# A Mamba block, an attention block and two expert layers: the hand-over into each expert search, and the first expert behind it

## The chip, the core and the metric

One core of a Trainium2 chip runs the whole program. The metric is the device time of one execution in microseconds (us); lower is better.

## The reference, cut to what matters

The input x is 16 sequences of 512 tokens with 256 channels, float32 (8192 tokens).

```python
x = x + mamba(layernorm(x))        # d_inner 512, 16 states, conv width 4
x = x + ffn(layernorm(x))
x = x + attention(layernorm(x))    # linear attention, 16 heads, chunks of 128
x = x + ffn(layernorm(x))

def ffn(x):                        # 8 experts, hidden 512
    capacity = n // 8              # 1024 tokens for each expert
    scores = (x_flat @ Wg.T).T     # (8, 8192): the gate products
    top_vals, token_idx = top_k(scores, capacity)
    token_w = softmax(top_vals)
    xg = x_flat[token_idx]
    h = silu(xg @ W1.T) * (xg @ W3.T)
    y = (h @ W2.T) * token_w[..., None]
    return zeros.at[token_idx].add(y)
```

## The kernel before

There are four stages: `mamba` (prefix m), `moe` (f), `attention` (t), `moe` (g). A counter `done` is raised at the end of each, and every engine waits for it before the next. The two layers with tokens in order (m, t) walk over the 16 batches (one sequence of 512 tokens each, four tiles of 128 tokens); the order of the work on every engine is written out by hand, and work of three neighbouring batches is interleaved: while batch b runs its scans or its attention, batch b-1 gets its output norm, its transposes and its gate products, and batch b+1 its input products. Behind each batch, `residual` adds the block's output to x, `out_norm1/2` (m) or `out_stats` (t) take mean and variance on VectorE, GpSimd makes `rstd` and `nm` of them in four small steps (a power and three others), ScalarE writes the normalized rows `xn1t`, TensorE transposes them (`ptr`), ScalarE copies the transposes out, and TensorE multiplies them with the gate's weights (`gate_scores`) into four groups of 32 partitions, one for each tile.

The search of `moe` wants the scores in another layout: `sc` has 128 partitions, partition 16e + b for expert e and batch b, with that batch's 512 tokens in a row. For batches 0 to 14 the scores go through HBM (`scores`), and `search.early`, issued from SyncE's queue near the end of m or t, loads them and the search's constants. In t it begins when the scores of batch 14 have landed in HBM, and behind it in the same queue stand the stores of the last batch (L1957, L1959). For batch 15, four DMAs (two from SyncE, two from ScalarE) take the scores from the last copy straight into `sc`; only when they have landed is `done` raised.

The search (`moe`) then bisects for the 1024th score of all experts at once: 16 rounds, each with three masks on VectorE (L1728), their sums on TensorE (L1611) and a few tiny VectorE steps. TensorE runs products that nobody reads (`unread`, L1378 and L2391) in between. At its start GpSimd makes an index table `numb` (128 x 2048) with an iota and a cast (L1440, L1443). Behind the search the slot numbers of expert 0 are made (`f_tok`, L1716), GpSimd issues eight gathers of 128 rows each (L1427), TensorE transposes the rows (L1564), ScalarE copies them out (L1480), and `hidden` runs eight parts of 512 tokens (L1586), each followed by a silu (ScalarE, L1495) and a product (VectorE, L1851). The first `hidden` waits for four gathers and four copies of transposes.

In the attention's `body` TensorE's order ends: `products(2)`, `ptr`, `values`, `earlier(2)`, `kt(0)`, `ptr`, `denominators`, `kt(1)`, `weighted(2)`, `project(0)`, `products(3)`, `spread`, `earlier(3)`, `tr`, `tr`, `kv01`, `gate_scores`, `weighted(3)`. Here `denominators` waits for ScalarE's copy of `kt(0)`, `spread` for VectorE's `residual(b, 0)`, `tr` for VectorE's `scale_q`, and `weighted(3)` for VectorE's `mask(3)`.

Of the kernel before, what the change touches and what calls it, by code (L numbers as in the profile page):

```python
# [137 lines left out]
Search = namedtuple("Search", "early last_scores landed all_landed constants warm tidy last")  # L138
# [23 lines left out]
def mamba(nc, done, x, x1, xn1, scores, bcd, ddd, w):  # L162


    with ExitStack() as stack:
# [67 lines left out]
                 "btr b_t dut du_t pr dA dBu dBp scan hD hP sum yg op x1 bs1 agg1 ve1 rstd1 nm1 xn1 pt ptev scm scev").split()  # L233
# [24 lines left out]
        def sync(sp_, search):  # L258
# [14 lines left out]
            def store_xn1(b):  # L273
                if b == NB - 1:
                    wait_alone(sp_, S["xn_h"], 2, S["tick"])
                else:
                    wait_alone(sp_, S["xn1"], b + 1, S["tick"])
# [122 lines left out]
            def epilogue():  # L400
# [5 lines left out]
                sp_.wait_ge(S["scev"], NB)  # L406
                for j in range(TJ // 2):
                    sp_.dma_start(search.last_scores[j], sc[j * SB:j * SB + NE, :]).then_inc(search.landed, 16)
# [8 lines left out]
        def scalar(act, search):  # L417
# [67 lines left out]
            def out_norm3(b, half):  # L485
# [7 lines left out]
                if half:  # L493
                    last.then_inc(S["xn1"], 1)
                elif b == NB - 1:
                    last.then_inc(S["xn_h"], 1)
# [173 lines left out]
            def epilogue():  # L670
                out_norm3(NB - 1, 0)
                pt_out(NB - 1, 0)
                sc_out(NB - 1)
                act.wait_ge(S["scev"], NB)
                for j in range(TJ // 2, TJ):
                    act.dma_start(search.last_scores[j], sc[j * SB:j * SB + NE, :]).then_inc(search.landed, 16)
# [3 lines left out]
        def gpsimd(pool):  # L680
# [80 lines left out]
            def epilogue():  # L761
                out_stats(NB - 1)
# [3 lines left out]
        def vector(dve):  # L766
# [134 lines left out]
            def epilogue():  # L901
# [4 lines left out]
                out_norm2(NB - 1)  # L906
                dve.wait_ge(S["nm1"], NB)
                dve.wait_ge(S["pt"], (NB - 1) * 2)
                dve.wait_ge(S["st_xn1"], (NB - 1) * 16)
                for j in range(2, TJ):  # L910
                    last = nc.vector.tensor_scalar(xn1t[:, j, :], x1t[:, j, :], rstd1[:, j:j + 1], nm1[:, j:j + 1],
                                                   ALU.mult, ALU.add)
                last.then_inc(S["xn_h"], 1)
                dve.wait_ge(S["pt"], NB * 2)
                nc.vector.tensor_copy(xnT[:, 1, :], wk[:, 1, :]).then_inc(S["ptev"], 1)
# [3 lines left out]
        def tensor(pe):  # L919
# [197 lines left out]

            def ptr(b, k, prep):
                if b == NB - 1:
                    pe.wait_ge(S["xn_h"], 2)  # L1120
                else:
                    pe.wait_ge(S["xn1"], b + 1)
# [62 lines left out]
            def body(b, par, post, prep):  # L1185
# [1646 lines left out]
```

## Time and profile before

| | |
|---|---|
| median of 3 runs | 3172.79 us (3171.89 to 3175.49) |
| profiled execution | 3173.42 us, its span 3171.6 us |
| busy share of the span | PE 86%, DVE 70%, POOL 66%, ACT 57% |
| chain that ended last | PE 53%, DVE 20%, issue 9%, POOL 7%, ACT 6%, DMA 5% |
| last work of m, first of f's search | 1739.71 to 1759.37 us |
| last work of t, first of g's search | 2709.95 to 2730.82 us |

PE is TensorE, PEld its weight loads, DVE VectorE, ACT ScalarE, POOL GpSimd, SP SyncE (SPq: its DMA issues). A float32 product counts as two records, a transpose or a bfloat16 product as one. PEclk is the granted share of TensorE's clock (1.00 is 2.4 GHz, 0.50 is 1.2 GHz). The profile is of one execution; its start is 0.

### The profile page before, as it was taken

Reading aid. Unit: us, or ns where it says so; the run is one execution under the profiler, and the core shown is the slowest. Engines: PE = TensorE matmul, PEld = TensorE weight load, DVE = VectorE, ACT = ScalarE, POOL = GpSimd, SP = SyncE. Lnnn points to the kernel's source line nnn. Section 1 sums busy time; section 2 is a strip of 40 time slices with the busy share of each in tenths; the row PEclk is TensorE's granted clock in tenths of the full one; section 3 lists DMA queues with packets and bytes.
Section 4 is the critical chain, followed back from the end, with each engine's and each line's share of the span. In section 5 each row is a group of like instructions: output and inputs, shape, how many; then the busy total and the mean of one; then the engine's idle time right before and its main releaser. Section 6 shows DMA issues by size and latency. Waiting matters only on the chain.

```text
span 3171.6 us, 47750 instructions
## 1 busy us (share of the span) xinstructions
PE 2742.0 (86%) x17112; PEld 1461.6 (46%) x17112; DVE 2231.3 (70%) x2384; ACT 1801.6 (57%) x3171; POOL 2088.8 (66%) x1301
## 2 busy tenths in 40 slices
PE   7788788877887888778866799998999999789999
PEld 3233233333332333233323456655677777455665
DVE  3999999999999999999999632221566666642211
ACT  4777877787877787777775022222555555122222
POOL 3899999999998999999997044444343433134553
PEclk9889898989998899888977899999999999899999
DMA  5556655665566556655562133333111111213442
GB/s 140 130 124 138 146 134 135 141 145 137 129 144 148 135 125 144 150 134 123 137 160 63 58 75 88 67 81 62 42 49 56 49 55 42 78 43 80 93 93 28
DMA packets 225385, 325.19 MB, mean 103 GB/s; under 512 B 40625, under 2 KB 116913, under 8 KB 225026
## 3 DMA queue, kind: packets, MB, share of 16 engines
q1 hardware_dynamic: 200514, 288.04, 36.6%
q0 software_dynamic: 24576, 34.10, 6.3%
q8 instruction: 140, 2.29, 0.3%
q14 instruction: 91, 0.75, 0.1%
q10 hardware_dynamic: 64, 0.02, 0.0%
HBM read 236.08 MB, written 85.95 MB: 102 GB/s over the span
## 4 chain that ended last, share of the span: by engine, by line
PE 53%; DVE 20%; issue 9%; POOL 7%; ACT 6%; DMA 5%; SPq 1%; DVEq 0%; ACTq 0%; POOLq 0%
PE t_wb L2383 9%; PE m_wk L921 9%; PE f_h L1586 7%; PE g_h L1586 7%; DVE m_pair L798 6%; DVE m_hc L798 4%; DMA m_bc<-bcd 4%; PE m_y L1018 4%; DVE m_hc L807 4%; PE g_yp L1600 3%; PE f_yp L1600 3%; POOL m_side L707 3%; POOL m_hc L716 2%; PE t_a_ps L2383 2%; PE t_num L2383 2%
## 5 line engine op out<-in xcount | busy, mean ns | idle before, releaser
L707 POOL TENSOR_TENSOR m_side<-m_du_r,m_bc 128x1024 f32<-128x1024 f32 x384 | 901.2, 2364 | 9.4 <-DMA m_du_r<-ddd 9.4
L716 POOL TENSOR_TENSOR m_hc<-m_hc,m_bc 128x1024 f32<-128x1024 f32 x224 | 527.6, 2358 | 115.3 <-DVE m_hc L798 113.6
L440 ACT ACTIVATE m_pair<-m_delta_r,m_a_neg 128x512 f32<-128x512 f32 x768 | 497.9, 680 | 179.7 <-DVE m_hc L807 94.2
L798 DVE TENSOR_TENSOR_SCAN m_pair<-m_pair,m_side 128x1024 f32<-128x1024 f32 x224 | 511.5, 2283 | 19.0 <-ACT m_pair L440 16.0
L1018 PE MATMUL m_y<-m_hc,m_fold 128*32 128x512 f32 x2048 | 326.9, 714 | 203.2 <-DVE m_hc L807 146.1
L798 DVE TENSOR_TENSOR_SCAN m_hc<-m_pair,m_side 128x1024 f32<-128x1024 f32 x160 | 362.8, 2276 | 10.4 <-ACT m_pair L440 5.9
L807 DVE TENSOR_TENSOR m_hc<-m_pair,m_bc 128x1024 f32<-128x1024 f32 x288 | 350.5, 1217 | 5.7
L921 PE MATMUL m_wk<-m_xnT,m_w_in 128*128 128x512 f32 x488 | 292.1, 729 | 23.3 <-DVE m_delta L783 23.3
L921 PE MATMUL m_wk<-m_xs,m_cw_diag 128*128 128x512 f32 x480 | 226.8, 605 | 10.1 <-ACT m_xs L510 10.1
L1851 DVE TENSOR_TENSOR g_hT<-g_sg,g_h 128x512 f32<-128x512 f32 x64 | 44.0, 687 | 256.7 <-ACT g_sg L1495 256.7
L1851 DVE TENSOR_TENSOR f_hT<-f_sg,f_h 128x512 f32<-128x512 f32 x64 | 44.0, 687 | 254.9 <-ACT f_sg L1495 254.9
L1586 PE MATMUL f_h<-f_xgT,f_w 128*128 128x512 f32 x512 | 221.8, 593 | 0.8 <-ACT f_xgT L1480 0.8
L1586 PE MATMUL g_h<-g_xgT,g_w 128*128 128x512 f32 x512 | 221.8, 593 | 0.8 <-ACT g_xgT L1480 0.8
L464 ACT ACTIVATE m_prod<-m_du_t,m_b_t 128x256 f32<-128x256 f32 x512 | 215.5, 496 | 4.0 <-PE m_pair L1074 3.1
L1018 PEld LDWEIGHTS m_y<-m_hc,m_fold 128*32 128x32 f32 x2048 | 45.7, 115 | 366.9 <-issue 366.8
L921 PEld LDWEIGHTS m_wk<-m_xnT,m_w_in 128*128 128x128 f32 x488 | 99.6, 227 | 218.7 <-issue 164.2
L1427 POOL DMA_INDIRECT f_xg<-xn,f_tok x64 | 64.3, 1005 | 196.7 <-DVE f_tok L1716 179.3
L1427 POOL DMA_INDIRECT g_xg<-xn,g_tok x64 | 64.0, 1001 | 196.9 <-DVE g_tok L1716 179.5
L798 DVE TENSOR_TENSOR_SCAN m_hc<-m_side,m_pair 128x1024 f32<-128x1024 f32 x64 | 146.0, 2282 | 37.3 <-issue 18.7
L440 ACT ACTIVATE m_side<-m_delta_r,m_a_neg 128x512 f32<-128x512 f32 x256 | 167.7, 711 | 0.0
L1074 PE MATMUL m_pair<-m_ident,m_prod 128*128 128x128 f32 x1024 | 140.4, 282 | 23.2 <-DVE m_hc L807 16.6
L1074 PEld LDWEIGHTS m_pair<-m_ident,m_prod 128*128 128x128 f32 x1024 | 121.1, 146 | 84.2 <-issue 84.2
(342 smaller groups left out, 5036.8 us busy)
## 6 DMA issues: line engine op xcount, KB each, us to landing
m_delta_r<-ddd SPq DMA_DIRECT2D x252, 256.0 KB, 6.6
m_du_r<-ddd SPq DMA_DIRECT2D x252, 256.0 KB, 7.5
m_bc<-bcd SPq DMA_DIRECT2D x192, 128.0 KB, 3.0
ddd<-m_delta SPq DMA_DIRECT2D x31, 512.0 KB, 3.0
ddd<-m_du SPq DMA_DIRECT2D x31, 512.0 KB, 3.8
f_w<-in_w SPq DMA_DIRECT2D x24, 512.0 KB, 6.1
g_w<-in_w SPq DMA_DIRECT2D x24, 512.0 KB, 6.0
m_xt<-in_x SPq DMA_DIRECT2D x16, 512.0 KB, 10.0
```

What stands on the lines that cost most here:

```text
L440: last = nc.scalar.activation(to, delta_r[:, c % 2, q, :], ACT.Exp, scale=a_neg[:, c * NQ + q, st:st + 1])
L464: last = nc.scalar.activation(prod[:, :, :, k, n * SB:(n + 1) * SB], du_t[:, k, :, :].rearrange("p c (h f d) -> p (c h) f d", h=2, d=SB), ...
L707: nc.gpsimd.tensor_tensor(side[:, un % RING, :, :], du_r[:, c % 2, 2 * h:2 * h + 2, :], bc[:, 0, st:st + 1, :].to_broadcast([P, 2, T]), AL ...
L716: nc.gpsimd.tensor_tensor(hc[:, un % RING, :, :], hc[:, un % RING, :, :], bc[:, 1, st:st + 1, :].to_broadcast([P, 2, T]), ALU.mult).then_i ...
L798: nc.vector.tensor_tensor_scan(to, decay, added, 0.0, ALU.mult, ALU.add).then_inc(S["scan"], 1)
L807: nc.vector.tensor_tensor(hc[:, un % RING, :, :], pair[:, un % 2, :].rearrange("p (i t) -> p i t", t=T), bc[:, 1, st:st + 1, :].to_broadca ...
L921: return nc.tensor.matmul(out, lhsT, rhs, start=first, stop=last)
L1018: last = nc.tensor.matmul(y[q * SB:(q + 1) * SB, c % 2, :], fold[:], hc[:, (2 * m + q // 2) % RING, q % 2, :], start=False, stop=st == NSE ...
L1074: last = nc.tensor.transpose(pair[:, un % 2, f * T + k * P:f * T + (k + 1) * P], prod[:, c % 2 * 2 + h, f, k, :], ident[:])
L1586: last = nc.tensor.matmul(out[:, m % 2, :], wt[:, q, k, f * P:(f + 1) * P], xgT[:, q, k, half * T:(half + 1) * T], start=k == 0, stop=k == ...
L1600: last = nc.tensor.matmul(yp[:, l % 2, 0:C], hT[:, half, f, j * P:(j + 1) * P], w2[:, e % 2, f, :], start=f == 0, stop=f == KF - 1)
L2383: return nc.tensor.matmul(out, lhsT, rhs, start=first, stop=last, **kw)
```

## The change

- Last batch of m and of t: `ve` and `nm` are made on VectorE, only the power stays on GpSimd; rows are normalized, transposed, copied out and multiplied in pairs of tiles (`ptr_last`, `gates_last`), in t with the statistics in pairs too (`stats_last`). In m VectorE has tiles 0 and 1 and ScalarE 2 and 3; in t ScalarE has 0, 1 and 3 and VectorE 2.
- The gate products of the last batch use a padded weight `w_pad` (128 x 256), in which only the columns 16e + 15 are not zero, so that they come out in PSUM in the layout of `sc`. Its partitions 16e + 15 are loaded with zeros, and VectorE adds the products to `sc` (`fill`). The four DMAs are gone. `early` has two more DMAs (`zero` and `g_W`, between the scores and `blk`).
- `unread` products are added: 10 before the last `total` of m and 12 behind its last `outp_last`, 3 and 8 in t's last batch, 20 to 30 before `compact(0)`; 26 become 22 before expert 0's transposes, 7 become 5 in `warm`.
- The index table: GpSimd makes 32 numbers, ScalarE spreads them to 128 x 2048.
- Expert 0: the first two gathers have a semaphore of their own; tokens 0 to 255 and 256 to 511 are transposed and multiplied apart for the first two hidden groups (10 parts in place of 8). The slot ranks of the other experts move behind part 1 on VectorE.
- The attention's order on TensorE, ScalarE and VectorE, in every batch (below), and `inv_std` of batch 0 as in the last batch.

```diff
@@ search.early
+            sp.dma_start(sc[NB - 1:P:NB, :], w["zero"]).then_inc(S["ld_sc"], 16)
+            sp.dma_start(w_pad[:], w["g_W"]).then_inc(S["ld_g"], 16)
             sp.dma_start(blk[:], w["blk"]).then_inc(S["ld_b"], 16)
+        def fill(dve, p, last_scores):
+            half = slice(p * T // 2, (p + 1) * T // 2)
+            dve.wait_ge(S["ld_sc"], 16 * (NE + 1))
+            nc.vector.tensor_tensor(sc[:, half], last_scores, sc[:, half], ALU.add).then_inc(S["filled"], 1)
@@ moe, gpsimd
-            nc.gpsimd.iota(numi[:], pattern=[[1, SB], [0, COLS]], ...)
+            nc.gpsimd.iota(numi[:], pattern=[[1, SB]], ...)
-            nc.gpsimd.tensor_copy(numb[:], numi[:]).then_inc(S["num_b"], 1)
@@ moe, scalar
+            nc.scalar.copy(numb[:], num32[:]...to_broadcast([P, SB, COLS])).then_inc(S["num_b"], 1)
@@ moe, parts of expert 0
+        FRONT = [(0, f, t, PAIRED) for t in (0, PAIRED) for f in range(2)] + [(0, f, 0, T) for f in range(2, KF)]
@@ mamba, tensor, last batch
+                    unread(10)
                     total(b, NM - 1)
             def epilogue():
                 for half in range(2):
                     outp_last(half, range(KD - 1, KD))
-                for k in range(KC):
-                    ptr(NB - 1, k, False)
-                gate_scores(NB - 1)
+                unread(12)
+                ptr_last(0)
+                ptr_last(1)
+                gates_last(0, search)
+                gates_last(1, search)
@@ attention, tensor, body
-                earlier(b, par, 2)
                 if not last:
                     kt(b + 1, 1 - par, 0)
+                earlier(b, par, 2)
...
+                weighted(b, par, 2)
+                if not last:
                     kt(b + 1, 1 - par, 1)
-                weighted(b, par, 2)
+                products(b, par, 3)
                 project(b, 0)
-                products(b, par, 3)
+                earlier(b, par, 3)
                 if not last:
                     spread(b + 1)
-                earlier(b, par, 3)
+                weighted(b, par, 3)
...
-                weighted(b, par, 3)
             def epilogue():
                 project(NB - 1, 1)
-                for k in range(2):
-                    ptr(NB - 1, k)
-                gate_scores(NB - 1)
+                ptr_last(0)
+                unread(3)
+                gates_last(0, search)
+                unread(8)
+                ptr_last(1)
+                gates_last(1, search)
@@ attention, vector, body
+                mask(b, 3)
                 residual(b, par, 0)
-                mask(b, 3, (0,))
@@ attention, scalar, body: y_out(b, 3) from the head of batch b + 1 to behind pair_values(b + 1)
@@ the end of m and of t, sync
-                sp_.wait_ge(search.landed, search.all_landed)
+                sp_.wait_ge(S["scm"], NB + 1)
```

## Rows read from the trace of the kernel before

**Rows 1.** Timeline of m's end: start us, us, engine, line, work, [idle before].
```profile
1733.70 1.07 PE L1018 MATMUL m_y<-m_hc,m_fold 128*32 128x512 f32 x8
...
1739.71 1.94 PE L1018 MATMUL m_y<-m_hc,m_fold 128*32 128x512 f32 x8 [2.16 <-DVE m_hc L807]
...
1742.45 3.78 PE L1091 MATMUL m_wk<-m_w_out,m_yg 128*128 128x256 f32 x8 [0.80 <-DVE m_yg L818]
1744.56 0.69 DVE L825 TENSOR_TENSOR m_xr<-m_wk,m_xr 128x512 f32<-128x512 f32 x1 [2.17 <-PE m_wk L1091]
...
1750.92 0.73 DVE L911 TENSOR_SCALAR m_xn1t<-m_xr,m_rstd,m_nm 128x256 f32<-128x256 f32 x2 [2.37 <-POOL m_nm L689]
1752.07 1.97 PE L1128 MATMUL m_wk<-m_ident,m_xn1t 128*128 128x128 f32 x8 [5.84 <-ACT m_xn1t L491]
...
1759.37 0.43 DVE L1742 COPY f_high<-f_sc 128x512 bf16<-128x512 bf16 x1 [3.98 <-SPq L413]
```

**Rows 2.** Windows of TensorE there: stretch, its length, PE busy, PEclk, DMA, GB/s.
```profile
1737.50:1739.00 1.50, 0.05 (x1) 1.00 0.00 0
1739.00:1740.50 1.50, 0.79 (x4) 0.70 0.00 0
```

**Rows 3.** Timeline of the first masks of f's search.
```profile
1759.41 2.23 POOL L1440 IOTA f_numi<- 128x2048 int32 x1 [8.52 <-SPq L413]
...
1759.83 1.95 DVE L1728 TENSOR_SCALAR f_seen<-f_high 128x512 bf16<-128x512 bf16 x1
...
1761.94 1.95 POOL L1443 CAST f_numb<-f_numi 128x2048 bf16<-128x2048 int32 x1
```

**Rows 4.** Groups by line: all later masks of that kind (busy us, mean ns).
```profile
L1728 DVE TENSOR_SCALAR f_seen<-f_high,f_trial 128x512 bf16<-128x512 bf16 x21 | 6.2, 350 | 0.2
```

**Rows 5.** Timeline of TensorE before f's expert 0.
```profile
1821.51 7.45 PE L1378 MATMUL f_tp<-f_blk_b 128*128 128x512 bf16 x26
...
1831.07 7.11 PE L1586 MATMUL f_h<-f_xgT,f_w 128*128 128x512 f32 x16 [0.82 <-ACT f_xgT L1480]
```

**Rows 6.** Chain of waits there: start us, us, what.
```profile
1826.17 2.94 DMA f_xg<-xn,f_tok
...
1839.05 10.30 PE f_h L1586 x24
```

**Rows 7.** Timeline of TensorE before g's expert 0.
```profile
2792.01 8.58 PE L1378 MATMUL g_tp<-g_blk_b 128*128 128x512 bf16 x26
```

**Rows 8.** Timeline of t's end: last products, SyncE's issues, first search step.
```profile
2709.95 1.12 PE L2383 MATMUL t_a_ps<-t_phiq,t_phim 32*128 32x128 f32 x32
...
2714.94 3.43 SPq L1357 DMA_DIRECT2D g_sc<-sc  x8
...
2723.78 0.38 SPq L1959 DMA_DIRECT2D xn<-t_xn1t  x1
...
2730.82 0.43 DVE L1742 COPY g_high<-g_sc 128x512 bf16<-128x512 bf16 x1 [10.33 <-SPq L1995]
```

**Rows 9.** DMA issues of 2715 to 2735 us: size, median us to landing.
```profile
xn<-t_xn1t SPq DMA_DIRECT2D x1, 512.0 KB, 3.0
g_blk<-in_blk SPq DMA_DIRECT2D x1, 64.0 KB, 1.8
```

**Rows 10.** What TensorE waited for, 2230 to 2696 us: total us, times, longest.
```profile
PE t_wb L2383 <- ACT t_phikt L2149: 6.6, 15, 0.9
PE t_wb L2399 <- DVE t_phiq L2273: 3.4, 14, 0.2
```

**Rows 11.** Timeline of one attention batch: denominators, project(0), residual, earlier(3).
```profile
2561.68 0.64 PE L2383 MATMUL t_wb<-t_zq,t_hsel 128*32 128x128 f32 x16 [0.43 <-ACT t_phikt L2149]
...
2563.42 2.00 PE L2383 MATMUL t_wb<-t_wp,t_yT 128*128 128x256 f32 x8
...
2565.45 0.69 DVE L2311 TENSOR_TENSOR t_xb<-t_wb,t_xb 128x512 f32<-128x512 f32 x1 [1.79 <-PE t_wb L2383]
...
2567.49 0.71 PE L2383 MATMUL t_num<-t_phiq,t_state 128*128 128x128 f32 x4
```

More of the change, by code:

```diff
@@ L137 @@
 Stage = namedtuple("Stage", "scope sync gpsimd scalar tensor vector")
-Search = namedtuple("Search", "early last_scores landed all_landed constants warm tidy last")
+Search = namedtuple("Search", "early fill padded constants warm tidy last")
 def turns(n, prologue, body, epilogue):
@@ L1341, in moe, with parts, parts_ahead, multiplied @@
         S = {n: s.sem(n) for n in
-             "ld_sc ld_b ld ldc one high rmax mrow emax emb mcol nmax cnt tot num trial found above offp offs small runs placed kept "
+             "ld_sc ld_g filled ld_b ld ldc one high rmax mrow emax emb mcol nmax cnt tot num trial found above offp offs small runs placed kept "
              "pos ex ext exo st_w ew isw sw rw slw tp posi loi hii lohi "
-             "iota num_b tile fold hot lhot lpart lval cp ev fd thi tok issued "
+             "iota num32 num_b tile fold hot lhot lpart lval cp ev fd thi tok issued "
              "ld0 ld1 tr xev h sg mul y ye".split()}
         S.update(by_pool)
-        g_base, sc_base = turn * 16 * TJ * (NE // 2), turn * NE * 16 * NSLOT
+        PAIRED = T // 2
+        FRONT = [(0, f, t, PAIRED) for t in (0, PAIRED) for f in range(2)] + [(0, f, 0, T) for f in range(2, KF)]
+        sc_base = turn * NE * 16 * NSLOT
+        def parts(e):
+            return (FRONT if e == 0 else [(0, f, 0, T) for f in range(KF)]) + [(1, f, 0, T) for f in range(KF)]
+        def parts_ahead(e):
+            return e * NH_ + (len(FRONT) - KF if e else 0)
+        def multiplied(e, half):
+            return parts_ahead(e + 1) - (HALVES - 1 - half) * KF
+        def gathered(e, half):
+            n = 16 * TJ * (turn * (NE // 2) + e // 2 + 1)
+            return n - 32 * (turn + 1) if e % 2 == 0 and half == 0 else n
         xn_e = xn[:, C:ROW].rearrange("(b j p) e -> p j b e", j=TJ, p=P)
@@ L1395, in warm @@
             pe.wait_ge(S["one"], 2)
-            unread(7)
-        search = Search(early, last_scores, S["ld_sc"], 16 * (NE + TJ), constants, warm, tidy, [S["y"], S["ye"]])
+            unread(5)
+        search = Search(early, fill, (w_pad, S["ld_g"]), constants, warm, tidy, [S["y"], S["ye"]])
         def sync(sp):
@@ L2188, in body @@
             def body(b, par, first, last):
-                if not first:
-                    y_out(b - 1, 3)
                 if not last:
@@ L2370, in body @@
                     scale_q(b + 1, 1 - par, 1)
-                mask(b, 3, (1,))
-                if not last:
                     keep01(b + 1)
@@ L2720, in arrange @@
         "g_P": np.pad(rows(ff["Wg"].T), ((0, 0), (0, 0), (0, 32 - NE))),
+        "g_W": np.stack([np.where(row[None, :] % NB == NB - 1, m[:, row // NB], 0) for m in rows(ff["Wg"].T).swapaxes(0, 1)], 1),
+        "zero": np.zeros((NE, T), np.float32),
         "odd": (row[:, None] // 16 % 2 == np.arange(2)[None, :]).astype(np.float32),
```

331 lines of the change are left out of this document (219 added, 112 removed).

## Prediction, made before the changed kernel ran

> **What bounds the kernel now.** I read the chain of waits first, then the timeline of the two places where it leaves the steady loops. In the loops it is TensorE (PE 53%, DVE 20%), and the change touches only the attention's. At m's end [rows 1] the work is serial: last sums at 1739.71, projection 1742.45, residual 1744.56, statistics, four GpSimd steps with VectorE idle 2.37 us until 1750.92, rows, transposes 1752.07, gate products, DMAs, and the search's first step at 1759.37. The row of 1739.71 takes 1.94 us where the same eight records took 1.07 at 1733.70: TensorE sat idle 2.16 us before, and PEclk falls to 0.70 and then 0.50 in the windows around it [rows 2]. The first search masks last 1.95 us beside GpSimd's iota and cast [rows 3], later ones 0.35 [rows 4]. Before expert 0 [rows 5, 6] the last of four gathers is issued at 1826.17 and lands 2.94 us later; TensorE starts at 1831.07. At t's end [rows 8] the last products start at 2709.95 and the search at 2730.82; SyncE issues the search's loads from 2714.94.
>
> **Part 1, m's end: 4.8 us.** (a) The 10 unread products fill the 2.16 us hole: at 2.4 GHz 512 columns take 0.21 us, so 2.1 us, done when the sums are due. Sums at full clock save 1.94 - 1.07 = 0.9. The projection's 3.78 halves to 1.9, but VectorE needs the first half: its residual starts 2.11 us behind the projection, 1.15 at full clock, and from there on it is bound by itself (0.69 + two statistics, twice), so 1.2 more less a residual wait of 0.2 that goes too. Together 2.1. (b) One tiny VectorE step before the power and one behind instead of three GpSimd steps: 2.37 becomes some 1.85, 0.5 less. (c) From `nm` (1750.92) to the search's first step there were 8.45 us. Now: two tiles on VectorE 0.73 + 0.15; a first set of four transposes, of which eight took 1.97 at half clock, so 0.8 to 1.0; then the second 1.0; the products of pair 0, four records of 256 columns, at the projection's half-clock rate (3.78/8) 1.9; of pair 1 1.0 to 1.9; `fill`, estimated at half of the 0.69 residual plus start, 0.4; hand-overs 0.3. That is 6.2 us, and 2.2 less than before. TensorE has idled over 3 us by then in spite of the 12 unread products, so I take half clock at first. At full clock it is 4.9 us, bound by TensorE; the store of the rows, issued behind VectorE's tiles and 3.0 us long like its like in t [rows 9], would then end almost with it. Range of part 1: 3.6 to 6.1. In m the two extra loads cost nothing: the queue is idle for 12 us behind them.
>
> **Part 2, index table: 3.1 us in each search, 6.2.** The long iota and cast are gone, so two masks go from 1.95 to 0.35: 3.2, less 0.1 for the order. ScalarE's spread of 128 x 2048, some 2 us, lies in a wait of over 20 us for the maxima. The small GpSimd steps left, below 0.3 us each, are over before the masks start where `fill` ends later than `done`; else each mask could lose up to 0.3, so the lower bound is 2.4 each. On the rows just cited: the Trainium skill ("SBUF — State Buffer", Who interferes with whom) says that a VectorE instruction in a two-port mode and a GpSimd one exclude each other for the whole instruction, whoever comes first. By that rule the short steps still hold a mask back, and the sum would be 0.3 to 0.7 less in a search where they coincide; it would be the same in the other.
>
> **Part 3, clock at the start of the search: 0.4 in f, 0.7 in g.** The unread products between rounds 0 and 1 run at half clock now and hold round 1's sums back by up to 0.9 us; TensorE comes in busier. Bounds 0 and 1.1.
>
> **Part 4, expert 0: 1.7 us in f, 2.6 in g.** Gathers are issued 1.27 us apart, so the second lands about 2.5 us before the fourth, at 1826.6. Then four transposes (0.6), one copy (0.6), part 0 of 256 columns: half of 7.11/2 = 3.55, 1.8 us, until 1829.8. The second set of transposes fits there with the rows just in (1829.11), its copy lies beside part 1, and parts 1 to 3 (three times 1.8) run to 1835.6; transposes of the other half (1.0) to 1836.6, where before the corresponding part started at 1839.05 [rows 6]: 2.4. The ranks of the other experts, 2.7 us on VectorE, stand before product 2, which ends at 1836.3, just before TensorE needs its buffer. The condition is that the unread products end before 1826.6. 22 at full clock do (4.7 us from 1821.51). 26 took 7.45 [rows 5], partly at half clock; at that clock 22 end at 1828.1 and 1.4 of the 2.4 are lost. In g 26 took 8.58 [rows 7], over a microsecond behind the rows, so there 3.3 and 1.9. The 10 more before `compact(0)` fill a hole of 2.4 us; I take the mean of both clocks. Behind this, expert 1's gathers shift with all else.
>
> **Part 5, t's end: 1.8 us.** This is the step that I think is worth least of what it looks. The new order puts the mask of the last tile first, so the last attention products end 1.5 us earlier; halves of statistics run beside the projection; and without a check on loads the last `fill` would end near 2722.9, 7.9 before 2730.82 [rows 8]. But `early` waits for the scores of batch 14, now behind `weighted(3)`: it starts at 2715.5 instead of 2714.94. Each issue takes 0.43 to 0.47 us of the queue (3.43 for eight), so `g_W`, the tenth, is issued at 2719.45 and lands 1.8 to 2.0 us later (1.8 at half its size [rows 9]), at 2721.4. The products of pair 0 were ready at 2717.3. TensorE's queue is in order, so 8 unread products (1.7 at full clock, 3.4 at half), the transposes and the products of pair 1 stand behind: 0.95 + 1.7 + 0.6 + 0.6 + 1.1 + 0.5 gives the first search step at 2727.1 at full clock, some 2731.0 at half after 4 us idle. The same queue ends `early` at 2722.7 with its 16 issues; then come the stores of x and of the rows (2723.3 instead of 2723.78), and `done` at 2726.4 to 2727.5. Bounds 3.7 gained and 0.2 lost; I take 2729.0, 1.8 gained, as the clock comes back within the stretch.
>
> **Part 6, the attention's order: 1.1 us.** 30.4 of a batch's 31.18 us are TensorE's own. Its waits are for the copy of `kt(0)` (0.43) and for `scale_q` (0.24) [rows 10], and less than 0.1 for another. With `kt(0)` ahead of `earlier(2)` the first falls to 0.2, with `weighted(3)` ahead of `tr` the second to 0.1. But `spread` overwrites the bank that `residual` reads, and residual starts 2.03 us behind `project(0)` and lasts 0.69 [rows 11], with 0.14 for the hand-over 2.86. Until now `products(3)` covered that; now only `project(0)`'s 1.93 and `earlier(3)`'s 0.5 [rows 11] do: a new wait of 0.4. I work out 0.08 us a batch for 14 batches. Bounds: 0.25 a batch gained or 0.1 lost, 3.5 and -1.5. Batch 0's `inv_std` gives 0: its transposes stand behind 20 unread products that end with it.
>
> **Sum.** f: 4.8 + 3.1 + 0.4 + 1.7 = 10.0. g: 1.8 + 3.1 + 0.7 + 2.6 = 8.2. With 1.1 it is 19.3 us. The profiled execution took 3173.4, so 3154.1; the median shown is 0.6 lower, and I predict 3153.5.
>
> **Rivals.**
> *The gate's weights are not late.* Then t's end gives 7.9 and not 1.8: 3147.4. It needs `early` to run before the last batch; for it speaks only that in m it does. The rows give the queue's issue times, against it. Chance 0.10. The skill's "DMA: Bandwidth & Descriptors" (Rules for kernel authors) says to issue a DMA early and to wait for it late, so that its fixed cost is hidden; by that rule this load would cost nothing, and here it is not issued early.
> *The attention's order takes away all its waits*, 0.76 us a batch, 10.6 in place of 1.1: 3144. Against it stands the wait behind residual. Chance 0.08.
> *The clock doesn't hold* under the added products: part 1 falls by 2.4, part 3 by 1.1, part 4 by 1.4, part 5 by 2.0, together 6.9: 3160.4. For it: a hole of 2.16 us was enough at 1739. Chance 0.15.
> *Slower: the attention's loop.* `spread` now waits for `residual`, which VectorE takes only behind both halves of `mask(3)`, and `weighted(3)`, ScalarE's `y_out` and the copies of `tr` hang on it in one row. If this ring, and not TensorE, sets the batch, the price repeats 14 times: from 1.46 us a batch (20.4/14) it eats the gain. At 2.0 us the time would be 3172.8 - 20.4 + 28 = 3180.4. My count leaves ScalarE 0.3 us of slack there. Chance 0.04.
>
> **How the numbers follow.** The forecast keeps 0.63. About 0.2% (6 us) is what a measurement of this kernel can tell from none. Forecast and the three fast rivals are faster but for their tails: 0.94; the slow one and its tail 0.03 slower, 0.03 within. The range takes in the clock rival and most of the bounds: all best terms together, with the clock falls inside the search (1.7 us, they shift by chance), give 3144, all worst 3163; I take 3145 to 3162.
>
> **What would show it.** The row of the last sums in m at 1.1 us; first masks at 0.35; from the last products of m to `high` 5 us less. In t: `g_W` issued some 4.5 us behind the first score load, TensorE idle before pair 0's products, and two to four microseconds gained, not eight. A batch of the attention at 31.1 us with a new wait on `residual` of 0.3 to 0.4. Expert 0's first full part 2.4 us earlier. Wrong would be a batch off 31.1 by over 0.3, or t's end giving over 5.

## The result, and the profile after

The changed kernel takes 3154.59 us (median of 5, 3152.52 to 3158.20), the one before 3172.97 in the same session: a ratio of 0.9943, 95% interval 0.9931 to 0.9954. That is 18.4 us faster; the prediction's sum was 19.3. The profiled execution has a span of 3152.8 us against 3171.6, so 18.8 us are to be found in the two traces. In the table each stage runs from one fixed point of the trace to the next, and the prediction's term stands beside it.

| stage | before, us | after, us | gain | predicted |
|---|---|---|---|---|
| start to the last sums of m | 1739.71 | 1740.45 | -0.7 | 0 |
| last sums to `f_high` | 19.7 | 14.25 | 5.4 | 4.8 |
| first masks, f and g | 4.64, 4.70 | 1.36, 1.35 | 3.3, 3.35 | 3.1 each |
| rest of the search to the token list, f | 57.0 | 56.9 | 0.1 | 0.4 |
| the same, g | 55.8 | 56.6 | -0.8 | 0.7 |
| token list to the row of 24 records of 512 tokens in expert 0, f | 17.9 | 15.2 | 2.7 | 1.7 |
| the same, g | 18.8 | 14.9 | 3.9 | 2.6 |
| attention's start | 62.1 | 63.4 | -1.3 | 0 |
| attention's loop, 13 batches | 405.4 | 402.1 | 3.3 | 1.1 |
| last batches to `g_high` | 64.1 | 63.0 | 1.1 | 1.8 |
| other experts, f and g | 360.2, 361.3 | 360.3, 362.8 | -1.5 | 0 |

The timeline of m's end in the changed kernel, its columns as in [rows 1]:

```profile
1740.45 1.07 PE L1026 MATMUL m_y<-m_hc,m_fold 128*32 128x512 f32 x8 [0.91 <-DVE m_hc L807]
...
1742.32 1.99 PE L1099 MATMUL m_wk<-m_w_out,m_yg 128*128 128x256 f32 x8 [0.80 <-DVE m_yg L818]
1743.49 0.69 DVE L825 TENSOR_TENSOR m_xr<-m_wk,m_xr 128x512 f32<-128x512 f32 x1 [1.22 <-PE m_wk L1099]
...
1748.67 0.74 DVE L917 TENSOR_SCALAR m_xn1t<-m_xr,m_rstd,m_nm 128x256 f32<-128x256 f32 x2
1749.46 1.09 PE L1139 MATMUL m_wk<-m_ident,m_xn1t 128*128 128x128 f32 x8 [2.56 <-DVE m_xn1t L917]
1750.80 3.35 PE L929 MATMUL m_y<-m_xnT,f_w_pad 128*128 128x256 f32 x8 [0.24 <-ACT m_xnT L674]
...
1754.70 0.47 DVE L1816 COPY f_high<-f_sc 128x512 bf16<-128x512 bf16 x1
```

Against [rows 1]: the sums are at 1.07 instead of 1.94, the projection at 1.99 instead of 3.78, the residual follows it by 1.17 instead of 2.11. The transposes run at full clock too, which I had not taken, and the gate products at half clock, which I had. The windows of TensorE (busy, granted clock, DMA, GB/s) show that the fall comes behind a hole of 2.56 us:

```profile
1742.40:1747.00 4.60, 4.50 (x20) 1.00 0.09 31
1747.00:1750.80 3.80, 1.10 (x9) 1.00 0.31 103
1750.80:1754.80 4.00, 4.00 (x11) 0.57 0.39 131
```

Of the masks, the one that took 1.95 in [rows 3] takes 0.29, and the rest of ScalarE's and GpSimd's new work lies beside. Expert 0 of f on TensorE, against [rows 5, 6]:

```profile
1813.41 4.91 PE L1440 MATMUL f_tp<-f_blk_b 128*128 128x512 bf16 x22
1818.40 0.66 PE L1636 MATMUL f_tp<-f_ident,f_xg 128*128 128x128 f32 x4
1819.83 1.97 PE L1661 MATMUL f_h<-f_xgT,f_w 128*128 128x256 f32 x8 [0.77 <-ACT f_xgT L1542]
...
1828.12 10.47 PE L1661 MATMUL f_h<-f_xgT,f_w 128*128 128x512 f32 x24
```

22 unread products at full clock end just as the two gathers are in, and the row of 24 records starts 15.2 us behind the token list. At t's end, against [rows 8]:

```profile
2702.44 3.43 SPq L1410 DMA_DIRECT2D g_sc<-sc  x8
2706.61 0.45 SPq L1413 DMA_DIRECT2D g_w_pad<-in_g_W  x1
...
2708.93 2.04 PE L2519 MATMUL t_a_ps<-t_xn1T,g_w_pad 128*128 128x256 f32 x4 [5.11 <-DMA g_w_pad<-in_g_W]
2710.77 3.41 PE L2527 MATMUL t_a_ps<-t_ident 128*128 128x512 bf16 x8
...
2711.57 0.38 SPq L2045 DMA_DIRECT2D xn<-t_xn1t  x1
...
2716.99 0.48 DVE L1816 COPY g_high<-g_sc 128x512 bf16<-128x512 bf16 x1
```

`g_W` is issued 4.17 us behind the first score load and lands 2.2 later, TensorE waits 5.11 us for it, and the products behind the wait run at half clock (8 unread in 3.41). In the attention's loop TensorE's two waits of [rows 10] are gone but for one execution of each, and one new wait of 0.43 a batch stands in their place:

```profile
PE t_wb L2519 <- DVE t_xb L2416: 6.0, 14, 0.4
```

The start of the attention lost 1.3 us by the landing of `t_ident`: 3.5 us from issue before, 5.2 after, and between 3.6 and 5.8 in five further traces of the changed kernel and its variants, so I take it for chance. The row of the other experts I take so too: one gather of expert 1 took 3.75 us to land where 2.8 is the median, and three variants traced on a chip of the same speed have 361.5 to 362.3 us in g.

### The profile page after: what moved, and what is told of

It reads as the page before. It is cut to its first block, busy times and chain, and to the rows that moved or that the text cites. A ratio compares the mean times of both kernels' runs of the same rounds, so it can differ in the third digit from the quotient of the medians.

```text
span 3152.8 us, 47869 instructions
## 1 busy us (share of the span) xinstructions
PE 2736.8 (87%) x17169; PEld 1470.3 (47%) x17169; DVE 2228.2 (71%) x2400; ACT 1806.4 (57%) x3175; POOL 2078.4 (66%) x1291
## 4 chain that ended last, share of the span: by engine, by line
PE 53%; DVE 19%; issue 9%; POOL 7%; ACT 6%; DMA 5%; SPq 1%; DVEq 0%; POOLq 0%; ACTq 0%
PE t_wb L2519 9%; PE m_wk L929 9%; PE g_h L1661 7%; PE f_h L1661 7%; DVE m_pair L798 6%; DVE m_hc L798 4%; DMA m_bc<-bcd 4%; PE m_y L1026 4%; DVE m_hc L807 4%; PE g_yp L1675 3%; POOL m_side L706 3%; PE f_yp L1675 3%; POOL m_hc L715 3%; PE t_a_ps L2519 2%; PE t_num L2519 2%
## 5 line engine op out<-in xcount | busy, mean ns | idle before, releaser
L798 DVE TENSOR_TENSOR_SCAN m_pair<-m_pair,m_side 128x1024 f32<-128x1024 f32 x224 | 511.4, 2283 | 19.7 <-ACT m_pair L438 16.5
L1929 DVE TENSOR_TENSOR f_hT<-f_sg,f_h 128x512 f32<-128x512 f32 (+1 forms) x66 | 44.3, 672 | 256.7 <-ACT f_sg L1560 256.7
L1929 DVE TENSOR_TENSOR g_hT<-g_sg,g_h 128x512 f32<-128x512 f32 (+1 forms) x66 | 44.3, 672 | 256.0 <-ACT g_sg L1560 256.0
L1661 PE MATMUL f_h<-f_xgT,f_w 128*128 128x512 f32 (+1 forms) x528 | 222.0, 580 | 0.8 <-ACT f_xgT L1542 0.8
L1661 PE MATMUL g_h<-g_xgT,g_w 128*128 128x512 f32 (+1 forms) x528 | 222.0, 580 | 0.8 <-ACT g_xgT L1542 0.8
```

What stands on the lines that cost most here:

```text
L798: nc.vector.tensor_tensor_scan(to, decay, added, 0.0, ALU.mult, ALU.add).then_inc(S["scan"], 1)
L1661: last = nc.tensor.matmul(out[:, m % 2, 0:n], wt[:, q, k, f * P:(f + 1) * P], xgT[:, q, k, half * T + t:half * T + t + n], start=k == 0, s ...
```

## Experiments

The kernels ran on several chips. On some of them every kernel took 0.8% longer (the kernel before 3196 to 3198 us), nearly all of it in the experts' stages: from f's token list to TensorE's first product of the attention it is 390 to 397 us there and 380 to 382 on the others, and from g's token list to the end 387 to 392 and 376 to 380. So times are compared by the gain over the kernel before in the same session, and the reasons by the length of a stage. The changed kernel's gain is 18.4 us on the first chip and 20.2 on a slower one. The 95% interval of such a gain reaches 4 to 5 us to either side. Where two gains differ by less, their times alone decide nothing, and the reading rests on the stages of the two traces.

**The changed kernel again.**

> The changed kernel again, unchanged, beside the others of this call. Theory A: its gain over the kernel before is the 18.4 us of the first runs within 3 us, and its stages are those of the first trace within 0.5 us, but for the stretch from the first count to the token list, which takes either 54.5 or 56.3 us, as TensorE's granted clock is held or falls inside it (each of the two values was seen twice or more so far for f's and g's search of the kernels that share this code). Theory B: the searches' lengths go with the kernel and not with the moment, and both are 56.3 us here as in its first trace.

Measured 3178.14 against 3198.36, ratio 0.9938 (0.9925 to 0.9952). The stages repeat: last sums to `f_high` 14.50, masks 1.40 and 1.36, last batches the same, a batch of the attention 30.92. From the first count to the token list 56.31 and 56.07 us, as in the first trace; that alone fits B too, and the kernels below had to decide.

**The old index table.**

```
-nc.gpsimd.iota(numi[:], pattern=[[1, SB]], ...)
+nc.gpsimd.iota(numi[:], pattern=[[1, SB], [0, COLS]], ...)
+nc.gpsimd.tensor_copy(numb[:], numi[:]).then_inc(S["num_b"], 1)
-nc.scalar.copy(numb[:], num32[:] ... to_broadcast([P, SB, COLS]))
```

> The changed kernel with only the index table put back: GpSimd writes it whole (an iota of 128x2048 and its cast) and ScalarE's copy over the columns goes. Theory A (the wide GpSimd work held VectorE's first masks): the stretch from the f_high cast to the end of the third mask is 4.7 us again in both searches (1.4 in the changed kernel), later masks are 0.3 us each as now, and the time rises by 3.3 per search, 6.6 in all. Theory B (something else shortened the first masks, such as the order of the loads at that place): the stretch stays at 1.4 and the time within 0.5 us of the changed kernel's 3154.6.

Measured 3184.26 against 3197.27, a gain of 13.0 beside 20.2. The stretch from the cast to the third mask is 4.44 us in f and 4.47 in g instead of 1.37: theory A, 3.1 a search. The timelines of GpSimd and VectorE of this kernel show more than the two traces did:

```profile
1755.12 1.95 POOL L1502 IOTA f_numi<- 128x2048 int32 x1 [6.08 <-SPq L411]
...
1757.50 1.92 POOL L1505 CAST f_numb<-f_numi 128x2048 bf16<-128x2048 int32 x1
```
```profile
1755.52 1.83 DVE L1814 COPY f_high<-f_sc 128x512 bf16<-128x512 bf16 x1
1757.38 0.29 DVE L1800 TENSOR_SCALAR f_seen<-f_high 128x512 bf16<-128x512 bf16 x1
1757.59 2.11 DVE L1800 TENSOR_SCALAR f_seen<-f_sc 128x512 bf16<-128x512 f32 x1
```

The cast of `high` (0.43 to 0.47 otherwise) begins inside GpSimd's iota and ends 0.28 us behind it; the mask that begins just before GpSimd's cast takes its normal 0.29; the next (0.43 otherwise) begins inside the cast and ends 0.28 behind it. So each wide GpSimd instruction holds one VectorE instruction to its own end. The Trainium skill ("SBUF — State Buffer", Who interferes with whom) has this as a rule of exclusion over the whole instruction; for the wide instructions the trace agrees, with 1.83 and 2.11 us. For the short ones it shows nothing of the kind: GpSimd's steps of 0.16 to 0.43 us in the changed kernel run beside masks of 0.28 to 0.29, and with its repetition and both searches the longest such mask is 0.36.

**No unread products in m.**

```
-                    unread(10)
-                unread(12)
```

> The changed kernel without the 10 unread products ahead of the last sums and the 12 ahead of the row transposes at the end of the Mamba stage. Theory A (they keep TensorE at its high clock over the holes, a gain of about 2.1): the last sums take 1.9 us instead of 1.07 and the output projection 3.8 instead of 2.0 again, the transposes 2.0 instead of 1.1, and from the last sums to f_high it takes 16.5 to 17.5 us instead of 14.3; the time rises by 2 to 3 us. Theory B (the clock would have been high there anyway, or the slower products are hidden): the stretch stays within 0.5 us of 14.3.

The stage went A's way but less far: 15.88 us instead of 14.25 to 14.5, where A asked for 16.5 and more. These are TensorE's rows:

```profile
1741.22 1.47 PE L1026 MATMUL m_y<-m_hc,m_fold 128*32 128x512 f32 x8 [3.07 <-DVE m_hc L807]
1743.48 3.78 PE L1099 MATMUL m_wk<-m_w_out,m_yg 128*128 128x256 f32 x8 [0.79 <-DVE m_yg L818]
1751.90 1.97 PE L1139 MATMUL m_wk<-m_ident,m_xn1t 128*128 128x128 f32 x8 [4.64 <-DVE m_xn1t L917]
1753.69 2.82 PE L929 MATMUL m_y<-m_xnT,f_w_pad 128*128 128x256 f32 x8
```

The sums took 1.47 where [rows 1] have 1.94, and the gate products 2.82 where the changed kernel's took 3.35, as the clock came back while they ran; so less was lost than A says. But the time did not rise: 3174.40 against 3197.27, a gain of 22.9 where the changed kernel has 20.2. The intervals overlap, so neither a loss nor a gain is shown. The trace says where the 1.5 us came back: f's search, from the first count to the token list, takes 54.68 us instead of 56.3, and g's 54.4 instead of 56.1. Why the searches were short was tested next.

**More unread products in the search.**

```
-            unread(5)
+            unread(9)
             pe.wait_ge(S["ldc"], 16 * len(later))
```

> The changed kernel with 9 unread products instead of 5 behind the last round of the search, where TensorE otherwise stands idle for 1.0 us and works little for about 3. Theory A (this gap lets the granted clock fall a few us later in some executions, 0.58 over 4 us in the changed kernel's f and g, which runs the placing products at half speed and costs 1.65 us per search): the stretch from the first count to the token list takes 54.5 us in both searches, and the time falls by up to 3.3 us. Theory B (the clock falls for another reason, whatever lies in that gap): one or both searches still take 56.3 us, or the products added come to stand in the way and each search takes 0.3 us longer.

Measured 3175.63 against 3198.36, a gain of 22.7. Both searches are short, 54.66 and 54.38 us. The windows of TensorE behind the last round of f's search, first of the changed kernel's second execution, then of this one:

```profile
1795.70:1799.70 4.00, 3.08 (x11) 0.69 0.00 0
1799.70:1803.70 4.00, 4.00 (x26) 0.88 0.02 4
```
```profile
1798.20:1802.20 4.00, 3.40 (x23) 1.00 0.00 0
1802.20:1806.20 4.00, 4.00 (x24) 1.00 0.02 4
```

With 5 unread products there, of 20 searches traced (10 executions) 9 of f and 6 of g took 56.0 to 56.4 us, 1 of f and 3 of g 54.4 to 54.7, and one of g 54.9, with a fall at its start. With 9 (three kernels) five took 54.4 to 54.7, and one of g 55.1, again with a fall at its start. So behind that gap the clock falls in most executions and not in all, what decides between them is open, and with four more products of 0.2 us it fell there in none of six. It can still fall later. In f of this kernel it did so behind the token list. There the changed kernel's 22 unread products took 4.91 us, and here:

```profile
1813.31 6.59 PE L1440 MATMUL f_tp<-f_blk_b 128*128 128x512 bf16 x22
```

The row of 24 records then came 16.55 us behind the token list instead of 15.2. Most of what f's search gained was lost again there, in this execution.

**Expert 0 as it was.**

```
-FRONT = [(0, f, t, PAIRED) for t in (0, PAIRED) for f in range(2)] + ...
+FRONT = [(0, f, 0, T) for f in range(KF)]
-    .then_inc(S["gf" if e == 0 and l < 2 else f"g{q}{l // TJ}"], 16)
+    .then_inc(S[f"g{q}{l // TJ}"], 16)
... (the transposes, copies and ranks of before with it)
```

> The changed kernel with expert 0 of both searches as it was: one count of all four gathers of a half, transposes of a column half over four token tiles, no parts of 256 tokens, the ranks of the other experts ahead of expert 0's parts; the 30 and 22 unread products of the change stay. Theory A (the gain comes from starting on two of the four gathers): from the token list to the end of the first 512 tokens of part 0 it takes 17.0 to 17.8 us again in f instead of 15.2, and 16.5 to 18.5 in g instead of 14.9; the time rises by 4 to 5 us. Theory B (the gain comes from the clock that the 30 unread products kept, so that the transposes and the first part ran at the high level): at most 1 us per search is lost, 2 in all.

Measured 3182.98 against 3197.27, a gain of 14.3, 5.9 less than the changed kernel's. From the token list to the row of 24 records it takes 19.5 us in f and 19.0 in g, against 15.2 and 14.9. Theory A, by a wait longer than it asked for:

```profile
1814.73 4.91 PE L1440 MATMUL f_tp<-f_blk_b 128*128 128x512 bf16 x22
1822.37 1.09 PE L1629 MATMUL f_tp<-f_ident,f_xg 128*128 128x128 f32 x8 [2.74 <-DMA f_xg<-xn,f_tok]
1824.29 8.78 PE L1650 MATMUL f_h<-f_xgT,f_w 128*128 128x512 f32 x16 [0.82 <-ACT f_xgT L1541]
```

Four gathers keep TensorE idle for 2.74 us behind the 22 unread products, the granted clock falls to 0.57 over the next 4 us, and the first part takes 8.78 us where [rows 5] have 7.11. Starting on two gathers saves the wait and the fall that follows from it. This is not quite the kernel before, though: there 26 unread products reached up to the rows [rows 5], and the same stretch took 17.9 us in f. So of the 4.3 us in f only 2.7 are the gain over the kernel before. The other 1.6 are most likely what the old expert 0 loses by having only 22; no run has it with 26.

**The order of the attention, in a two by two.** The keys' transposes (`kt`) can stand old or new, and so can the end of the batch (projection, weighted 3, `spread`, the masks and ScalarE's copy).

```
keys new:  kt(0), earlier(2), ptr, denominators, weighted(2), kt(1)
keys old:  earlier(2), kt(0), ptr, denominators, kt(1), weighted(2)
end new:   products(3), project(0), earlier(3), spread, weighted(3), tr, ...
end old:   project(0), products(3), spread, earlier(3), tr, ..., weighted(3)
```

> The changed kernel with the whole old order inside attention's batches (TensorE's, VectorE's masks of product 3, ScalarE's copy of y 3), the last batch as changed. Theory A (the order gave 0.26 us a batch, 3.3 to 3.6 in all, more than the 1.1 that the prediction took): the period of a batch is 31.18 us again instead of 30.92 and the time rises by 3.3 to 3.6 us. Theory B (the gain of the loop comes from elsewhere, such as the tile xn's new place): the period stays at 30.9 and the time within 0.5 us.

> The changed kernel with only the keys' transposes put back on TensorE's queue (the first behind the earlier part of product 2, the second behind the denominators and ahead of weighted 2); the projection ahead of earlier 3, weighted 3 ahead of the transposes of the batch after next, and the orders of VectorE and ScalarE stay new. Theory A (the keys' move is what takes the wait for phi k out, and gives about 0.15 of the 0.26 us a batch): the period is 31.05 to 31.10 and the wait of TensorE for the keys' copy, 6.6 us in 15 times before, is back. Theory B (the whole gain is in the end of the batch): the period stays at 30.92.

> The changed kernel with the keys' transposes where the change puts them, and the rest of attention's batch in the old order (the projection ahead of product 3, weighted 3 last on TensorE's queue, VectorE's masks of product 3 in two parts around the scaling of q behind the residual, ScalarE's copy of y 3 in the next batch); the last batch as changed. The kernel with only the keys put back took 7.4 us more from attention's start to g_high than the changed kernel, the one with the whole old order 4.1 more. Theory A (the two parts of the move add up: the keys are worth 7.4 and the new end of the batch costs 3.3): this kernel is 3.3 us faster than the changed one, 512.8 us from attention's start to g_high instead of 516.1, with the wait for the residual gone and a small one for the scaled q (0.2 a batch) back. Theory B (the new end of the batch is what makes room for the keys' gain, without it the next wait takes it): at 516 to 520 us, no faster than the changed kernel.

| keys, end | period of a batch, us | waits of TensorE, us a batch | gain over the kernel before |
|---|---|---|---|
| old, old (the kernel before) | 31.17 | keys 0.43, q 0.24 | |
| old, old (in the changed kernel) | 31.18 | keys 0.40, q 0.24 | 16.4, beside 20.2 |
| old, new | 31.45 | keys 0.4, residual 0.43 | 14.0, beside 20.2 |
| new, old | 31.24 | keys 0.55, q 0.25 | 14.9, beside 18.4 |
| new, new (the changed kernel) | 30.92 | residual 0.43 | |

The waits of TensorE within the loop (what, total us, times, longest), old and old in the changed kernel; keys old, end new; keys new, end old:

```profile
PE t_wb L2525 <- ACT t_phikt L2244: 5.2, 13, 0.4
PE t_wb L2541 <- DVE t_phiq L2381: 3.4, 14, 0.2
```
```profile
PE t_wb L2519 <- DVE t_xb L2416: 5.6, 13, 0.4
PE t_wb L2519 <- ACT t_phikt L2244: 5.3, 13, 0.4
```
```profile
PE t_wb L2525 <- ACT t_phikt L2244: 7.2, 13, 0.6
PE t_wb L2541 <- DVE t_phiq L2381: 3.2, 13, 0.2
```

The old order's waits were predicted by A of the first run and came. My theory of the third, that the two parts add up, fell: it was to be 3.3 us faster and is 3.5 slower than the changed kernel. With the end old, the projection stands right behind `kt(1)` and needs the bank that ScalarE has not copied yet:

```profile
2552.95 0.44 PE L2583 MATMUL t_wb<-t_ident,t_phik 128*128 128x128 f32 x2
2553.94 1.97 PE L2525 MATMUL t_wb<-t_wp,t_yT 128*128 128x256 f32 x8 [0.55 <-ACT t_phikt L2244]
```

In the changed kernel `products(3)`, 1.12 us in another bank, stands between. The old wait of the denominators is gone in both: each half of the move takes away one old wait, and makes a new one, of 0.55 behind the keys and 0.43 behind the residual, of which the other half covers the first. Each half of the change alone makes the batch longer (31.45, 31.24) and both together shorter. TensorE's own work is the same in all, some 30.5 us, and what the waits add to it gives the period within 0.12.

**The constants of g's search ahead of the stores.**

```
 def body(b, par, first, last):
     ...
+    if last:
+        search.early_constants(sp)   # zero, g_W, blk, step, ident, low, part, fold
     if not first:
         store(b - 1, 1 - par)
```

> The changed kernel, but in attention's last batch SyncE issues the loads of the search's constants (the zero rows, the padded gate weights g_W, blk, step, ident, low, part, fold) a batch earlier, ahead of the stores of batch 14; only the 8 loads of the scores stay behind them. Theory A (the late load of g_W is what held gates0 for 5.1 us, and the row stores behind the constants' issues end the stage): gates0 starts at about 2704.5 instead of 2708.9 (relative to the changed kernel's trace), the row stores are issued 3 to 4 us earlier, and from project(14,1) to g_high it takes 27 to 29 us instead of 33.5; the time falls by 5 to 6 us. Theory B (the chain through the norms and ScalarE's copies, or the score loads, ends the stage, the load being late beside it): g_high comes at most 2 us earlier.

Measured 3170.59 against 3197.27, a gain of 26.7, 6.5 above the changed kernel's 20.2. From project(14,1) to `g_high` 28.25 us instead of 33.5: theory A. SyncE, TensorE and VectorE:

```profile
2698.32 0.45 SPq L1414 DMA_DIRECT2D g_w_pad<-in_g_W  x1
...
2715.75 4.57 SPq L1409 DMA_DIRECT2D g_sc<-sc  x8
...
2717.21 1.13 PE L2522 MATMUL t_a_ps<-t_xn1T,g_w_pad 128*128 128x256 f32 x4
...
2721.02 0.38 SPq L2046 DMA_DIRECT2D xn<-t_xn1t  x1
...
2725.03 0.43 DVE L1817 COPY g_high<-g_sc 128x512 bf16<-128x512 bf16 x1 [2.26 <-SPq L2084]
```

The products of pair 0 now follow the unread ones without a wait, and the end of the stage is the landing of the row store. The other 1.2 us of the 6.5 lie in g's search, 54.9 instead of 56.1. This is the largest gain of a single further change. It also puts a number on the rule that the prediction quotes (the Trainium skill, "DMA: Bandwidth & Descriptors", Rules for kernel authors: issue early, wait late): 5.3 us for loads issued a batch earlier.

**A longer cover of the hole instead.**

```
                 ptr_last(0)
-                unread(3)
+                unread(20)
```

> The changed kernel with 20 unread products instead of 3 between attention's last two groups of row transposes, while TensorE waits for the late load of the padded gate weights. Theory A (the wait of 5.1 us let the granted clock fall, and at the low level gates0 took 2.04 us and the 8 unread products 3.41): gates0 takes 1.1 to 1.2, the 8 unread products 1.7, and g_high comes 1.5 to 2.5 us earlier, where the landing of the row store ends the stage next. Theory B (the load and the stores end the stage whatever the clock): g_high comes within 0.5 us of the changed kernel's 33.5 us from project(14,1).

Measured 3151.69 against 3173.00, a gain of 21.3, 2.9 more than the changed kernel's. From project(14,1) to `g_high` 31.1 us:

```profile
2712.58 4.48 PE L2527 MATMUL t_a_ps<-t_ident 128*128 128x512 bf16 x20
2718.38 1.10 PE L2519 MATMUL t_a_ps<-t_xn1T,g_w_pad 128*128 128x256 f32 x4 [1.32 <-DMA g_w_pad<-in_g_W]
2719.32 1.89 PE L2527 MATMUL t_a_ps<-t_ident 128*128 128x512 bf16 x8
```

The load is as late as in the changed kernel and 2.4 us are gained all the same: 0.94 in the products, 1.5 in the eight behind. So of the stage's loss against an early load, under half is the clock.

**All together.** The constants early, the store of x ahead of the score loads and the rows' between them, 22 unread products instead of 12 in m, 9 instead of 5 in the search.

> The changed kernel with what the earlier runs point to: the constants of g's search loaded ahead of batch 14's stores, batch 15's x3 store ahead of the score loads and its row store between the fifth and sixth of them; 22 unread products instead of 12 at the end of the Mamba stage, which fill the 2.56 us in which TensorE waited for the rows; 9 instead of 5 behind the last round of each search. Theory A (each of the parts acts where it was seen): from project(14,1) to g_high 26 to 27.5 us instead of 33.5; the Mamba stage's gate products at the high level, 1.9 us instead of 3.35, and f_high 12.9 to 13.3 us behind the last sums instead of 14.3; both searches at 54.5 us. In all 9 to 11 us below the changed kernel (ratio to the kernel before 0.9903 to 0.991). Theory B (what is gained in one place is lost in the next: the earlier row store collides, the clock falls elsewhere): less than 6 us.

Measured 3144.62 us against 3173.00, ratio 0.9906 (0.989 to 0.9923): 28.4 us below the kernel before and 10.0 below the changed one. m's end is 12.92 us, with the gate products at 1.99; f's search 54.68, g's 55.1. Two parts missed: g's search, with a fall of the clock at its start, and t's end, 28.55 us instead of 26 to 27.5, no better than without the shuffling of the stores. SyncE's issues and VectorE's wait show where:

```profile
2702.03 4.13 SPq L1409 DMA_DIRECT2D g_sc<-sc  x5
...
2706.77 1.90 SPq L1409 DMA_DIRECT2D g_sc<-sc  x3
```
```profile
2710.12 0.76 DVE L1427 TENSOR_TENSOR g_sc<-t_a_ps,g_sc 128x256 f32<-128x256 f32 x2 [5.14 <-DMA g_sc<-sc]
```

These are eight loads of unequal length: six took 0.40 to 0.51 us each to issue, one took 2.25 (from 2702.58 on) and one 0.90. Such a long issue stands at t's end in every kernel traced here but the kernel before and the one with the longer cover: 1.36 at the store of x in the changed kernel, 1.54 at the fourth score load with the constants early. In the changed kernel it cost nothing, as TensorE's products ended the stage; with the constants early it held the row store back by 1.1; here it held every load behind it back, and the fills waited for the last. Without what the two took beyond 0.40, some 2.3 us, the stage would have taken about 26.2 (an estimate from these rows), as A says. What makes an issue long is open.

**The score loads on two queues.**

```
                 search.early_scores(sp, range(3))
...
                 pt_last(0)
+                search.early_scores(act, range(3, 5))
                 norm_last((3,), NB + 1)
+                search.early_scores(act, range(5, 8))
                 pt_last(1)
```

> The combined kernel with the end of attention changed once more: batch 15's stores stand behind three score loads on SyncE's queue, and the other five score loads are issued by ScalarE, two ahead of its last normalization and three ahead of its last copy, where it waits 1.2 and 1.6 us anyway; g's search has 10 unread products ahead of it instead of 5. In the combined kernel the eight loads took 6.0 us to issue on SyncE's queue around the stores, and their landing ended the stage (the fills waited 5.1 us for them). Theory A (the issue on one queue is the bound): from project(14,1) to g_high 26 to 26.8 us instead of 28.5, g's search 54.5 us instead of 55.1, and 2 to 3 us below the combined kernel's 3144.6 (ratio to the kernel before 0.990 to 0.991 becomes 0.9895 to 0.990). Theory B (the loads land late because they wait behind each other or behind the store of the scores of batch 14, or ScalarE's issues delay its chain): 28 us or more from project(14,1) to g_high, and no gain over the combined kernel.

Measured 3166.54 against 3196.26, ratio 0.9899 (0.9883 to 0.9916), a gain of 29.7; the combined kernel's interval holds that too. By stages: t's end 27.5 us, 1.1 better and short of the 26 to 26.8, g's search 54.43. ScalarE's two loads took as long as five at 0.40, and pushed its normalization back by 0.4; one of the two is long (1.35 us), beside one of 1.56 at the store of x on SyncE's queue:

```profile
2711.09 2.05 ACTq L1409 DMA_DIRECT2D g_sc<-sc  x2
...
2713.20 2.02 ACTq L1409 DMA_DIRECT2D g_sc<-sc  x3
```

## Why the prediction was right, step by step

The total came within 1.1 us, and that close it is luck. Three terms gave 4.5 us more than they were put at (the attention's order 2.2, expert 0 1.0 and 1.3), and three stages gave some 4.4 less (g's search 1.5, the attention's start 1.3, the other experts 1.6), two of which the prediction put at nothing and which I take for chance. The kinds of gain and of wait were right but for the points below.

- *m's end*, 4.8 against 5.4: right in mechanism. Of the clock part (a), the residual started 1.2 behind the projection as said; undoing both covers cost 1.6 in one trace, against the 2.1 of (a), as the sums and the gate products lost less there. The stretch from the rows to the search took 6.0 us where the sum said 6.2, the transposes at full clock, the gate products at half. The rest is the shorter path through the power. Neither the pairs of tiles nor the padded weight in place of four DMAs was undone by a run: their share is read from the two traces.
- *Index table*, 3.1 against 3.3: right, and shown by undoing it. The doubt about the short steps cost nothing.
- *Clock at the start of the search*, 0.4 and 0.7: the start gave this (0.5 and 0.9 from the masks to the count of round 1), and g's search lost 1.7 again to a fall of the clock behind its last round, which g of the kernel before had been spared. There the fall came behind the token list instead, in the 26 unread products of [rows 7], so part of g's larger gain in expert 0 is this same fall in another place. The prediction had it only as chance in its range; the runs showed its place, and that four more products keep it out of that place.
- *Expert 0*, 1.7 and 2.6 against 2.7 and 3.9: mis-sized. I took the mean of both clocks for the 22 unread products; they ran at full clock in both searches, and the 2.4 and 3.3 of the full-clock case were the better numbers. The other case was no empty fear: with 9 unread products in the search, the 22 of f took 6.59 us and the row of 24 came 1.4 later, which is the price that the prediction had for it. That the 30 products ahead hold the clock is thus not shown.
- *t's end*, 1.8 against 0.8 (1.1 with the last batch): mis-sized by 0.7 to 1.0. Counted from project(14,1), the products of pair 0 started some 0.5 us later than the 2721.4 of the sum. And of "as the clock comes back within the stretch" only the end held: the products of pair 0 and the 8 unread ran at half clock (2.04 and 3.41 us), and it was back for the transposes and pair 1 (0.60 and 1.13). The sum for full clock also adds up to 2726.85 and not 2727.1, which changes nothing. The rest of the step held, the late `g_W` above all, which the kernel with early constants put at 5.3 us and the one with a longer cover split into load and clock.
- *The attention's order*, 1.1 against 3.3: the new wait behind the residual came at 0.43 a batch as predicted (0.4). What failed is the rest that I left on the two old waits, 0.2 and 0.1: both went to nothing, and the batch gained 0.25 where the sum had 0.08. Nor had I seen the wait that the keys' move makes at the projection, 0.55 with the end old, which `products(3)` covers: the parts of the move work only together.
- Of the rivals, *weights not late* was a true price in the wrong kernel (5.3 us, where the rival said 6.1), *the clock doesn't hold* was half true, in t only, and neither *the order takes all waits* nor the slower *ring* happened. The ring's price was summed wrongly: the other parts give 18.2 us and not 20.4, so the batch would eat them from 1.3 us on, and at 2.0 us the time would be 3182.6.

Not settled: why the experts' stages take 10 us more on some chips (in the second trace of the changed kernel ScalarE's steps for `f_yo` wait 12 times, 22.6 us in all, for something that the trace does not name, in the first not once), what makes one DMA issue at t's end long, and why the Mamba stage ended 10 us later in the profiled execution of the kernel with the longer cover (3161 us, its others 3150 to 3152).

## What to carry to other kernels

Where work is moved between batches, list for each bank who writes it next and who must have read it, and price each wait with all moves in place: here each half of a reordering lengthened the batch and both shortened it. A load that the end of a stage needs belongs ahead of the stores of the batch before it, since there it cost no more than its place in the queue. And a hole of TensorE is to be priced with the clock that it loses behind it, which can show only a few records later: behind the 2.56 us at m's end the transposes still ran at full clock, and the gate products did not.

## What the runs showed of the hardware

- One wide GpSimd instruction (1.92 to 1.95 us) held one VectorE instruction of 0.4 us until its own end; a mask that started just before it ran in 0.29, and beside steps of 0.16 to 0.43 us masks ran in 0.28 to 0.36.
- The granted clock fell to its lower level behind holes of 2.2 to 5.1 us, and also behind 3 us of thin work with idle stretches of 1.0 us; there not always, but in 15 of 20 searches. Behind it products took twice as long, for some 3 to 7 us in these places.
- A DMA issue on SyncE's queue at t's end mostly took 0.3 to 0.65 us, but in all but two of the 14 traces one of them took 1.4 to 2.3, now a load and now a store. Five on ScalarE's queue took 0.47 to 1.35.
